# Inverse square roots of the norms: from VectorE's Newton chain to one GpSimd power instruction

## The chip, the core and the metric

The kernel runs on one core of a Trainium2 chip. The metric is the device time of one execution in microseconds (us). The core has TensorE (matrix products into PSUM), VectorE and ScalarE (which read PSUM and SBUF), GpSimd (SBUF only) and SyncE, which here only issues DMAs. The engines run side by side, each takes its own instructions in order, and they wait for each other on semaphores.

## What is computed

The input is 8 sequences of 512 tokens of 128 numbers. The model adds four residual parts: a full attention, a "local" stack, a second full attention and a gated mix. The change lies in the local stack, six layers of this (16 heads of 64, windows of 32 tokens):

```python
qkv = shift_tokens(x) @ Wqkv
q = q / max(norm(q), 1e-12) * q_scale          # per token and head
k = k / max(norm(k), 1e-12) * k_scale
q = rotate(q) * scale ; k = rotate(k) / scale  # rotary tables
attn = softmax(mask(8.0 * q @ k_window_and_previous.T))
x = (attn @ v) @ Wo + x
xn = (x - mean) / sqrt(var + 1e-5) * g + b     # of shift_tokens(x)
x = a * gelu(gate) @ W2 + b2 + x               # a, gate = split(xn @ W1 + b1)
```

Every token and head needs 1/norm(q) and 1/norm(k), and every token 1/sqrt(var + 1e-5). All of them are computed as inverse square roots of sums of squares.

## The kernel before

`local_stack` keeps the activations of all 8 sequences in SBUF and goes through 6 layers; for each layer it runs a loop over the 8 batches. One pass of that loop is called a body here, 48 of them in all, and each runs four chunks c = 0 to 3 of four heads each. The order of the work of each engine is written out by hand inside `body`, one for each engine. A chunk is a software pipeline: while the q and k of chunk c are made, the norms, broadcast and scores belong to chunk c-1, the softmax to c-2 and the value products to c-3, across the border of bodies too. The output product, the layernorm and the feed-forward part of the batch before (`prev`) go into chunks 2 and 3.

The steps of one chunk, with their lines and their engines:

- TensorE makes q (L1021) into the PSUM tile R[0], then k (L1034) into R[1], the sums of squares for each head (L1047, tiny products with `block4`) into R[3], v (L1062) into R[2], the scores (mask L1070, products L1074) into R[3], the transposes that broadcast the inverse norms (L1085, in chunk 3 also L1091) into R[0], in chunk 2 most of the output product (L1011), and the value products (L1112) into R[1]. In chunk 3 the feed-forward products (L1125, L1131) follow. `claim` makes it wait until the last reader of a tile has let go of it.
- ScalarE squares q and k (L821, L823), copies v (L829), spreads the inverse norms `rn` to `rnx` (L834), takes the exponential (L842) and copies the attention output (L849).
- VectorE rotates q (L890, `rotate(0)`), takes the norms out of PSUM (L926, in chunk 3 also L929), transposes the probabilities (L903), runs `rsqrt` (L87 to L96) on `norm`, rotates k (L890, `rotate(1)`), takes row maxima (L941), subtracts them (L943), scales the rotated q and k by the broadcast inverse norms (L954 twice, to `qn` and `kn`), and sums and inverts the softmax rows (L959, L961). `rsqrt` is a magic-number start with three Newton steps: 11 instructions that each wait for the one before. Both norms' instructions have a wait of VectorE for itself behind them, after which `norm_read` is raised.
- GpSimd forms the rotated halves from `t` into `u` (L792, L793) for q and for k, adds the squares (L794, L795), and multiplies the probabilities by the inverse sums (L801). `rotate` waits in `halves_of_pool` for `ra_ready` before it writes `t` again.
- SyncE issues eight DMAs that lay the transposed probabilities into a banded tile (L764 to L768, `pbd`) and eight for kn (L775, `kbd`).

VectorE lets TensorE have a PSUM tile again by a drain with a semaphore behind the last read (r0_dve and r1_dve in `rotate`, r3_dve behind L943, r0_dve_b behind L954; the drain at L956 is that one).

Of the kernel before, what the change touches and what calls it, by code (L numbers as in the profile page):

```python
# [11 lines left out]
ALU = mybir.AluOpType  # L12
# [3 lines left out]
D = 128  # L16
NB = 8
T = 512
NT = T // 128
LN_EPS = 1e-5  # L20
# [16 lines left out]
CH = H // NC  # L37
# [611 lines left out]
def local_stack(nc, C, xs, A):  # L649
# [8 lines left out]
    with ExitStack() as ctx:  # L658
        def sb(n, shape, dt=F32):
# [21 lines left out]
        ntmp = sb("ntmp", [D, NT * 2 * CH + NT])  # L681
        rn = sb("rn", [D, NT * 2 * CH + NT])
        NSS = NT * 2 * CH
# [17 lines left out]
                 "r2_act r0_dve r1_dve r3_dve rq_ready ra_ready sq_sum ss_ready norm_read rn_ready rnx_ready b_ready r0_dve_b "  # L701
# [81 lines left out]
        @block.gpsimd  # L783
        def _(pool):
            def body(par, l, start, b, prev):
                seen = Tally()
                for c in range(NC):
                    buf = c % 2
                    if b is not None:
                        for a in range(2):  # L790
                            pool.wait_ge(S["rq_ready"], seen.next(S["rq_ready"]))
                            nc.gpsimd.tensor_tensor(u[buf][:, 2 * a, :], t[:, 0, :], t[:, 3, :], ALU.subtract)  # L792
                            nc.gpsimd.tensor_tensor(u[buf][:, 2 * a + 1, :], t[:, 2, :], t[:, 1, :], ALU.add).then_inc(S["ra_ready"], 1)  # L793
                        nc.gpsimd.tensor_tensor(sqs[0][:], sq[0][:, 0, :], sq[0][:, 1, :], ALU.add)  # L794
                        nc.gpsimd.tensor_tensor(sqs[1][:], sq[1][:, 0, :], sq[1][:, 1, :], ALU.add).then_inc(S["sq_sum"], 1)  # L795
                        pool.drain().then_inc(S["sq_free"], 1)
                    if c == NC - 1:
                        seen.settle(pool)
                    if live(c, 2, b, prev):
                        pool.wait_ge(S["rec_ready"], seen.next(S["rec_ready"]))  # L800
                        nc.gpsimd.tensor_tensor(p[:], p[:], srec[:].unsqueeze(2).to_broadcast([D, NT * CH, 2 * WIN]),  # L801
                                                ALU.mult).then_inc(S["pn_ready"], 1)
                seen.settle(pool)

            layers(pool, body)
# [55 lines left out]
        def _(v):  # L861
# [11 lines left out]
            def body(par, l, start, b, prev):  # L873
# [12 lines left out]
                def rotate(a):  # L886
# [9 lines left out]
                    v.drain().then_inc(S["r0_dve"] if a == 0 else S["r1_dve"], 1)  # L896
# [9 lines left out]
                for c in range(NC):  # L906
# [15 lines left out]
                    if has_ss or has_var:  # L922
                        v.wait_ge(S["ss_ready"], seen.next(S["ss_ready"]))
                        lo, hi = (0 if has_ss else NSS), (NSS + NT if has_var else NSS)
                        if has_ss:
                            nc.vector.tensor_scalar(norm[:, 0:NSS], R[3][:, 0, 0:NSS], 1e-24, None, ALU.max).then_inc(S["step"], 1)  # L926
                            v.wait_ge(S["step"], seen.next(S["step"]))
                        if has_var:
                            nc.vector.tensor_scalar(norm[:, NSS:], R[3][:, 1, 0:NT], LN_EPS, None, ALU.add).then_inc(S["step"], 1)  # L929
                            v.wait_ge(S["step"], seen.next(S["step"]))  # L930
                        v.sem_inc(S["norm_read"], 1)
                    transpose_p(c)
                    if has_ss or has_var:
                        rsqrt(nc, v, seen, S["step"], norm[:, lo:hi], ntmp[:, lo:hi], rn[:, lo:hi]).then_inc(S["rn_ready"], 1)
# [3 lines left out]
                    if live(c, 2, b, prev):  # L938
# [6 lines left out]
                        v.drain().then_inc(S["r3_dve"], 1)  # L945
# [4 lines left out]
                    if has_ss:  # L950
# [5 lines left out]
                        v.drain().then_inc(S["r0_dve_b"], 1)  # L956
# [454 lines left out]
```

## Time and profile before

| | |
|---|---|
| median of 3 runs | 5786.65 us (5783.74 to 5801.6) |
| profiled execution, whole | 5801.78 us |
| its span, first to last instruction | 5800.0 us |
| TensorE busy (matmul) | 4979.5 us (86%) |
| TensorE weight loads | 2765.5 us (48%) |
| VectorE busy | 4089.1 us (71%) |
| ScalarE busy | 2198.8 us (38%) |
| GpSimd busy | 2000.6 us (34%) |
| mean granted TensorE clock | 0.929 |

The profiled execution has 1.8 us around its span. It took 15 us more than the median of the runs.

Three kinds of views are used below. The table of stretches has, for each stretch (start:end in us from the span's start), its length, the busy time of each engine with the number of instructions in it (in the order PE, PEld, DVE, ACT, POOL), the granted TensorE clock, the DMA engines' busy share and GB/s. PE is TensorE, PEld its weight loads, DVE VectorE, ACT ScalarE, POOL GpSimd. The timeline gives start, duration, engine, line, operation, output and inputs, count, and in brackets the idle time of the engine before it and what released it. The groups of instructions give the count, the busy time, the mean duration in ns, the idle time before and what ended it. The page's chain that ended last reaches only into the last few us of the program and says nothing about the local stack.

### The profile page before, as it was taken

To read this page: it belongs to the slowest core of one execution; us is meant where nothing else is said; L and a number is where in the kernel's file an instruction comes from. 1 tells how busy PE (TensorE), PEld (TensorE's weight loads), DVE (VectorE), ACT (ScalarE), POOL (GpSimd) and SP (SyncE) were. 2 spreads that over 40 slices of the span, in tenths; PEclk is the share of its full clock that TensorE was granted. 3 is DMA by queue.
4 is the path that set the end of the run, shared out by engine and by line. 5 is a ranking of instruction groups with operands and counts; after the bars stand their busy time and mean duration, and the time that the engine had idled before them with its cause. 6 is when DMAs were issued, how large, how long until landed. Compare 5 with 4: busy or idle time off the path is not lost. (4 is left out here: it accounts for less than half of the span.)

```text
span 5800.0 us, 90682 instructions
## 1 busy us (share of the span) xinstructions
PE 4979.5 (86%) x33904; PEld 2765.5 (48%) x34096; DVE 4089.1 (71%) x5868; ACT 2198.8 (38%) x2794; POOL 2000.6 (34%) x1547
## 2 busy tenths in 40 slices
PE   5999688898998999998898998998898998478886
PEld 2222255555555555555555555555555554222223
DVE  4677377777777777777777777777777776366652
ACT  0666333333333333333333333333333332035564
POOL 1111144444444444444444444444444442111110
PEclk6999799999999999999999999999999999579997
DMA  2222111112211122111222112112121111122210
GB/s 58 49 47 44 55 46 48 46 46 61 55 46 49 48 58 58 45 47 47 63 49 49 46 48 69 45 48 50 43 58 48 45 49 47 43 45 45 43 26 16
DMA packets 181029, 279.66 MB, mean 48 GB/s; under 512 B 58032, under 2 KB 79792, under 8 KB 174896
## 3 DMA queue, kind: packets, MB, share of 16 engines
q1 hardware_dynamic: 180880, 277.66, 19.5%
q8 instruction: 94, 1.54, 0.1%
q14 instruction: 55, 0.45, 0.0%
HBM read 61.70 MB, written 17.56 MB: 14 GB/s over the span
## 5 line engine op out<-in xcount | busy, mean ns | idle before, releaser
L792 POOL TENSOR_TENSOR l_u<-l_t 128x512 f32<-128x512 f32 x384 | 486.9, 1268 | 2110.3 <-DVE l_t L890 2110.3
L890 DVE SCALAR_TENSOR_TENSOR l_t<-l_r,l_qkvec,l_tab 128x1024 f32<-128x1024 f32 x768 | 949.3, 1278 | 294.5 <-ACT l_sq L821 291.3
L470 DVE TENSOR_REDUCE a_nmax<-a_pair 128x2 f32<-128x1024 f32 x512 | 612.4, 1221 | 374.5 <-PE a_pair L550 372.5
L1074 PE MATMUL l_r<-l_kbd,l_qn 128*32 128x256 f32 x12288 | 774.5, 390 | 44.5 <-DMA l_kbd<-l_kn 11.3
L388 ACT ACTIVATE a_pt<-a_st 128x512 f32<-128x512 f32 x1024 | 579.8, 597 | 335.4 <-PE a_st L534 325.3
L1021 PE MATMUL l_r<-xs,l_wqkv 128*128 (+1 forms) x768 | 431.9, 690 | 222.4 <-DVEq L956 189.0
L1074 PEld LDWEIGHTS l_r<-l_kbd,l_qn 128*32 128x32 f32 x12288 | 422.9, 111 | 302.2 <-issue 152.8
L1112 PE MATMUL l_r<-l_pbd,l_va 128*64 128x160 f32 (+1 forms) x6144 | 443.4, 297 | 127.7 <-DMA l_pbd<-l_pt 127.7
L534 PE MATMUL a_st<-a_qs,a_ks 75*128 75x512 bf16 x1024 | 391.7, 398 | 146.0 <-ACT a_pt L388 75.5
L801 POOL TENSOR_TENSOR l_p<-l_p,l_srec 128x1024 f32<-128x1024 f32 x192 | 365.3, 1903 | 415.6 <-DVE l_srec L961 284.7
L1112 PEld LDWEIGHTS l_r<-l_pbd,l_va 128*64 128x64 f32 x6144 | 400.2, 138 | 193.1 <-DVEq L896 108.3
L793 POOL TENSOR_TENSOR l_u<-l_t 128x512 f32<-128x512 f32 x384 | 489.2, 1274 | 0.0
L842 ACT ACTIVATE l_p<-l_p 128x1024 f32<-128x1024 f32 x192 | 203.1, 1058 | 721.5 <-DVE l_p L943 721.5
L1062 PE MATMUL l_r<-l_wqkv,l_xc 128*128 128x256 f32 x1536 | 424.7, 425 | 0.0
L1047 PEld LDWEIGHTS l_r<-l_block,l_sqs 128*128 128x128 f32 x3072 | 372.8, 192 | 97.7 <-issue 94.9
L550 PE MATMUL a_pair<-a_ks,a_qs 72*128 72x512 bf16 x1024 | 341.3, 419 | 83.0 <-DMA a_qs<-a_scr 59.7
L829 ACT ACTIVATE l_va<-l_r 128x1024 f32<-128x1024 f32 x192 | 196.7, 1024 | 546.0 <-PE l_r L1062 546.0
L821 ACT ACTIVATE l_sq<-l_r 128x1024 f32<-128x1024 f32 x192 | 196.6, 1024 | 538.3 <-PE l_r L1021 529.9
L1034 PE MATMUL l_r<-xs,l_wqkv 128*128 (+1 forms) x768 | 396.7, 642 | 3.0 <-DVEq L896 2.7
L534 PEld LDWEIGHTS a_st<-a_qs,a_ks 75*128 75x128 bf16 x1024 | 95.5, 97 | 561.1 <-ACT a_pt L388 429.0
L1047 PE MATMUL l_r<-l_block,l_sqs 128*128 128x4 f32 x3072 | 354.1, 247 | 1.4 <-POOL l_sqs L795 1.3
L834 ACT ACTIVATE l_rnx<-l_rn 128x1024 f32<-128x1024 f32 x192 | 203.3, 1059 | 380.5 <-DVE l_rn L96 380.5
(183 smaller groups left out, 7475.3 us busy)
## 6 DMA issues: line engine op xcount, KB each, us to landing
l_kbd<-l_kn SPq DMA_DIRECT2D x1536, 64.0 KB, 2.0
l_pbd<-l_pt SPq DMA_DIRECT2D x1344, 64.0 KB, 2.0
a_ks<-a_scr SPq DMA_DIRECT2D x96, 192.0 KB
a_qs<-a_scr SPq DMA_DIRECT2D x288, 64.0 KB
a_scr<-a_parts SPq DMA_DIRECT2D x48, 256.0 KB, 2.5
l_wqkv<-in_wqkv SPq DMA_DIRECT2D x6, 1536.0 KB, 6.9
l_pbd<-l_pt SPq DMA_DIRECT2D x192, 48.0 KB, 1.9
l_wo<-in_wo SPq DMA_DIRECT2D x6, 512.0 KB, 3.7
```

The costliest lines, as they stand in the source:

```text
L388: nc.scalar.activation(pt[n % 2][:, r, :], st[r % 2][:], ACT.Exp, scale=SC).then_inc(exp_done, 1)
L470: nc.vector.tensor_reduce(out=nmax[:, n, 2 * i:2 * i + 2], in_=pair[i][:], op=ALU.max, axis=AX.X, negate=True).then_inc(pair_dve[i], 1)
L534: nc.tensor.matmul(st[r % 2][:], ks[1 - par][0:ROWS, h, 128 * kt:128 * kt + 128], qs[1 - par][0:ROWS, h, :], start=True, stop=True).then_i ...
L792: nc.gpsimd.tensor_tensor(u[buf][:, 2 * a, :], t[:, 0, :], t[:, 3, :], ALU.subtract)
L793: nc.gpsimd.tensor_tensor(u[buf][:, 2 * a + 1, :], t[:, 2, :], t[:, 1, :], ALU.add).then_inc(S["ra_ready"], 1)
L890: last = nc.vector.scalar_tensor_tensor(out=t[:, 2 * half:2 * half + 2, :], in0=R[a][:, half, :].unsqueeze(1).to_broadcast([D, 2, T]), sca ...
L1021: last = nc.tensor.matmul(R[0][:, half, :], wqkv[par][:, o:o + D], xs[:, b, 0:T], start=True, stop=True)
L1034: last = nc.tensor.matmul(R[1][:, half, :], wqkv[par][:, o:o + D], xs[:, b, 0:T], start=True, stop=True)
L1047: last = nc.tensor.matmul(R[3][:, 0, o:o + CH], sqs[a][:, 128 * k:128 * k + 128], block4[:], start=True, stop=True)
L1062: last = nc.tensor.matmul(R[2][:, k // 2, 256 * (k % 2):256 * (k % 2) + 256], xc[:, 128 * k:128 * k + 128], wqkv[par][:, o:o + CH * DH], s ...
L1074: last = nc.tensor.matmul(R[3][q:q + 32, bank, 256 * (w // 4):256 * (w // 4) + 256], qn[:, half, WIN * W:WIN * W + WIN], kbd[half][:, :, W ...
L1112: last = nc.tensor.matmul(R[1][q:q + 64, bank, 128 * g:128 * g + WIN * span], va[cc][:, g, DH * h:DH * h + DH], pbd[c % 2][:, 0:span, o:o ...
```

## The change

A GpSimd instruction, `tensor_tensor` with ALU.pow, raises `norm` to -0.5, element by element, straight into `rn` (128x32, in chunk 3 128x36, in the tail 128x4). Its second operand is a tile of -0.5, filled once by a memset. It stands between GpSimd's halves of q and of k and waits for the new semaphore `norm_ready`, which VectorE raises with the last norm instruction. The 11 VectorE instructions of `rsqrt`, their waits and the tile `ntmp` are gone from the local stack (the layernorm passes outside keep theirs), and so are the two waits of VectorE for its own norm instructions; `norm_read` is raised by an engine no-op. The four drains of a chunk are replaced by engine no-ops that raise the same semaphores.

```diff
--- before.py
+++ after.py
@@ -678,8 +678,8 @@
         qn, kn = sb("qn", [D, 2, T]), sb("kn", [D, 2, T])
         kbd = [sb(f"kbd{i}", [D, CH, KC]) for i in range(2)]
         norm = sb("norm", [D, NT * 2 * CH + NT])
-        ntmp = sb("ntmp", [D, NT * 2 * CH + NT])
         rn = sb("rn", [D, NT * 2 * CH + NT])
+        minus_half = sb("minus_half", [D, NT * 2 * CH + NT])
         NSS = NT * 2 * CH
         rnx = sb("rnx", [D, NSS, HALF])
         p = sb("p", [D, NT * CH, 2 * WIN])
@@ -698,7 +698,7 @@
         R = [ctx.enter_context(nc.psum_tensor(f"l_r{i}", [D, 2, T], F32)) for i in range(4)]
 
         names = ("late_pe late_act late_dve late_free wqkv_free qkvec_free consts_pe consts_dve xc_ready q_dve q_act k_dve k_act v_act sq_free "
-                 "r2_act r0_dve r1_dve r3_dve rq_ready ra_ready sq_sum ss_ready norm_read rn_ready rnx_ready b_ready r0_dve_b "
+                 "r2_act r0_dve r1_dve r3_dve rq_ready ra_ready sq_sum ss_ready norm_read norm_ready rn_ready rnx_ready b_ready r0_dve_b "
                  "qn_ready kn_ready kbd_full s_ready t_ready p_ready rec_ready pn_ready pt_ready pt_free pbd_free "
                  "va_ready pv_ready ot_ready wo_ready x_ready mean_ready centred fsq_ready bc_ready xng_ready "
                  "xnf_ready g_ready a_ready gelu_ready h_ready f_ready ffn_done step pstep init mask_full").split()
@@ -782,12 +782,26 @@
 
         @block.gpsimd
         def _(pool):
+            nc.gpsimd.memset(minus_half[:], -0.5).then_inc(S["pstep"], 1)
+            pool.wait_ge(S["pstep"], 1)
+
             def body(par, l, start, b, prev):
                 seen = Tally()
+
+                def inverse_roots(has_ss, has_var):
+                    lo, hi = (0 if has_ss else NSS), (NSS + NT if has_var else NSS)
+                    pool.wait_ge(S["norm_ready"], seen.next(S["norm_ready"]))
+                    nc.gpsimd.tensor_tensor(rn[:, lo:hi], norm[:, lo:hi], minus_half[:, lo:hi], ALU.pow).then_inc(S["rn_ready"], 1)
+
                 for c in range(NC):
                     buf = c % 2
+                    has_ss, has_var = live(c, 1, b, prev), c == 3 and prev is not None
+                    if b is None and (has_ss or has_var):
+                        inverse_roots(has_ss, has_var)
                     if b is not None:
                         for a in range(2):
+                            if a == 1 and (has_ss or has_var):
+                                inverse_roots(has_ss, has_var)
                             pool.wait_ge(S["rq_ready"], seen.next(S["rq_ready"]))
                             nc.gpsimd.tensor_tensor(u[buf][:, 2 * a, :], t[:, 0, :], t[:, 3, :], ALU.subtract)
                             nc.gpsimd.tensor_tensor(u[buf][:, 2 * a + 1, :], t[:, 2, :], t[:, 1, :], ALU.add).then_inc(S["ra_ready"], 1)
@@ -893,7 +907,7 @@
                                                               in1=tab[:, 2 * a:2 * a + 2, :], op0=ALU.mult, op1=ALU.mult)
                     last.then_inc(S["rq_ready"], 1)
                     unread["ra"] = 1
-                    v.drain().then_inc(S["r0_dve"] if a == 0 else S["r1_dve"], 1)
+                    nc.vector.engine_nop().then_inc(S["r0_dve"] if a == 0 else S["r1_dve"], 1)
 
                 def transpose_p(c):
 
@@ -921,17 +935,13 @@
                     has_ss, has_var = live(c, 1, b, prev), c == 3 and prev is not None
                     if has_ss or has_var:
                         v.wait_ge(S["ss_ready"], seen.next(S["ss_ready"]))
-                        lo, hi = (0 if has_ss else NSS), (NSS + NT if has_var else NSS)
                         if has_ss:
-                            nc.vector.tensor_scalar(norm[:, 0:NSS], R[3][:, 0, 0:NSS], 1e-24, None, ALU.max).then_inc(S["step"], 1)
-                            v.wait_ge(S["step"], seen.next(S["step"]))
+                            last = nc.vector.tensor_scalar(norm[:, 0:NSS], R[3][:, 0, 0:NSS], 1e-24, None, ALU.max)
                         if has_var:
-                            nc.vector.tensor_scalar(norm[:, NSS:], R[3][:, 1, 0:NT], LN_EPS, None, ALU.add).then_inc(S["step"], 1)
-                            v.wait_ge(S["step"], seen.next(S["step"]))
-                        v.sem_inc(S["norm_read"], 1)
+                            last = nc.vector.tensor_scalar(norm[:, NSS:], R[3][:, 1, 0:NT], LN_EPS, None, ALU.add)
+                        last.then_inc(S["norm_ready"], 1)
+                        nc.vector.engine_nop().then_inc(S["norm_read"], 1)
                     transpose_p(c)
-                    if has_ss or has_var:
-                        rsqrt(nc, v, seen, S["step"], norm[:, lo:hi], ntmp[:, lo:hi], rn[:, lo:hi]).then_inc(S["rn_ready"], 1)
                     if b is not None:
                         v.wait_ge(S["k_dve"], seen.next(S["k_dve"]))
                         rotate(1)
@@ -942,7 +952,7 @@
                         v.wait_ge(S["step"], seen.next(S["step"]))
                         nc.vector.tensor_tensor(p[:], sc, smax[:].unsqueeze(2).to_broadcast([D, NT * CH, 2 * WIN]),
                                                 ALU.subtract).then_inc(S["t_ready"], 1)
-                        v.drain().then_inc(S["r3_dve"], 1)
+                        nc.vector.engine_nop().then_inc(S["r3_dve"], 1)
                     if has_var:
                         v.wait_ge(S["bc_ready"], seen.next(S["bc_ready"]))
                         nc.vector.scalar_tensor_tensor(out=xng[:], in0=xcn[:], scalar=vec[:, 4:5], in1=R[2][:, 0, :],
@@ -953,7 +963,7 @@
                         for a, (dst, ready) in enumerate(((qn, "qn_ready"), (kn, "kn_ready"))):
                             nc.vector.tensor_tensor(dst[:], u[par1][:, 2 * a:2 * a + 2, :],
                                                     R[0][:, a, :].unsqueeze(1).to_broadcast([D, 2, T]), ALU.mult).then_inc(S[ready], 1)
-                        v.drain().then_inc(S["r0_dve_b"], 1)
+                        nc.vector.engine_nop().then_inc(S["r0_dve_b"], 1)
                     if live(c, 2, b, prev):
                         v.wait_ge(S["p_ready"], seen.next(S["p_ready"]))
                         nc.vector.tensor_reduce(out=ssum[:], in_=p[:], op=ALU.add, axis=AX.X).then_inc(S["step"], 1)
```

## Rows read from the trace of the kernel before

**Rows 1.** The page, first section: busy time and share of the span.

```profile
PE 4979.5 (86%) x33904; PEld 2765.5 (48%) x34096; DVE 4089.1 (71%) x5868; ACT 2198.8 (38%) x2794; POOL 2000.6 (34%) x1547
```

**Rows 2.** Table of stretches, the whole local stack.

```profile
695.50:4937.00 4241.50, 3804.60 (x28590) 2363.32 (x28782) 3227.13 (x4902) 1480.96 (x1530) 1798.93 (x1344) 0.96 0.20 50
```

**Rows 3.** Table of stretches, chunks 0 to 3 of one body.

```profile
4619.56:4637.61 18.05, 14.68 (x138) 9.93 (x137) 15.33 (x23) 7.38 (x7) 7.47 (x6) 1.00 0.11 28
4637.61:4655.77 18.16, 14.79 (x137) 10.04 (x139) 15.31 (x23) 6.10 (x6) 9.38 (x7) 1.00 0.23 57
4655.77:4675.80 20.03, 19.80 (x150) 12.19 (x151) 16.79 (x25) 5.18 (x5) 9.62 (x8) 1.00 0.23 56
4675.80:4705.31 29.51, 28.51 (x175) 16.74 (x175) 20.17 (x31) 12.22 (x14) 11.03 (x8) 0.94 0.20 50
```

**Rows 4.** Timeline of TensorE in chunk 1 of that body.

```profile
4637.61 1.98 PE L1021 MATMUL l_r<-xs,l_wqkv 128*128 x4 [2.02 <-DVEq L956]
...
4647.20 1.97 PE L1074 MATMUL l_r<-l_kbd,l_qn 128*32 128x256 f32 x32
4649.25 1.09 PE L1085 MATMUL l_r<-ident,l_rnx 128*128 128x128 f32 x8
4651.44 2.29 PE L1112 MATMUL l_r<-l_pbd,l_va 128*64 128x160 f32 x32 [1.10 <-DMA l_pbd<-l_pt]
4655.77 1.99 PE L1021 MATMUL l_r<-xs,l_wqkv 128*128 x4 [2.04 <-DVEq L956]
```

**Rows 5.** Timeline of VectorE in the same chunk.

```profile
4643.37 0.19 DVE L926 TENSOR_SCALAR l_norm<-l_r 128x32 f32<-128x32 f32 x1
...
4644.95 0.91 DVE L87 TENSOR_SCALAR l_ntmp<-l_norm 128x32 int32<-128x32 int32 x1
...
4647.91 0.19 DVE L96 SCALAR_TENSOR_TENSOR l_rn<-l_ntmp,l_rn 128x32 f32<-128x32 f32 x1
4648.02 2.47 DVE L890 SCALAR_TENSOR_TENSOR l_t<-l_r,l_qkvec,l_tab 128x1024 f32<-128x1024 f32 x2
4650.63 1.23 DVE L941 TENSOR_REDUCE l_smax<-l_r 128x16 f32<-128x1024 f32 x1
...
4653.32 1.22 DVE L954 TENSOR_TENSOR l_qn<-l_u,l_r 128x1024 f32<-128x1024 f32 x1 [0.21 <-POOL l_u L793]
4654.46 1.21 DVE L954 TENSOR_TENSOR l_kn<-l_u,l_r 128x1024 f32<-128x1024 f32 x1
```

**Rows 6.** One line's instructions: min/median/max ns, the chain's first.

```profile
L87 DVE TENSOR_SCALAR l_ntmp<-l_norm x193: 139/901/923, 717.4 to 4933.4; 128x32 int32<-128x32 int32 x145, 128x36 int32<-128x36 int32 x47, 128x4 int32<-128x4 int32 x1
```

**Rows 7.** Timeline of GpSimd, chunk 1: the second half of q and k.

```profile
4644.54 1.28 POOL L793 TENSOR_TENSOR l_u<-l_t 128x512 f32<-128x512 f32 x1
...
4651.79 1.28 POOL L793 TENSOR_TENSOR l_u<-l_t 128x512 f32<-128x512 f32 x1
```

**Rows 8.** Timeline of SyncE's queue, start of chunk 1: kn's DMAs.

```profile
4637.54 4.94 SPq L775 DMA_DIRECT2D l_kbd<-l_kn  x8
```

**Rows 9.** Timelines of GpSimd, TensorE and VectorE in chunk 3.

```profile
4686.89 1.27 POOL L793 TENSOR_TENSOR l_u<-l_t 128x512 f32<-128x512 f32 x1
...
4690.86 1.97 PE L1074 MATMUL l_r<-l_kbd,l_qn 128*32 128x256 f32 x32
...
4693.01 1.23 DVE L941 TENSOR_REDUCE l_smax<-l_r 128x16 f32<-128x1024 f32 x1
```

**Rows 10.** Table of stretches, chunks 1 and 2 of another body.

```profile
2541.04:2560.72 19.68, 16.42 (x138) 10.64 (x139) 15.32 (x23) 6.10 (x6) 9.37 (x7) 0.91 0.21 53
2560.72:2582.29 21.57, 21.42 (x149) 12.77 (x151) 16.12 (x25) 5.19 (x5) 10.47 (x8) 0.92 0.23 57
```

**Rows 11.** Groups of GpSimd's instructions: a two-input one and the shortest.

```profile
L801 POOL TENSOR_TENSOR l_p<-l_p,l_srec 128x1024 f32<-128x1024 f32 x192 | 365.3, 1903 | 415.6 <-DVE l_srec L961 284.7 <-POOLq L63 130.9
...
L1403 POOL MEMSET const-float32-0.0<- 128x1 f32 x1 | 0.1, 104 | 0.3 <-issue 0.3
```

**Rows 12.** Timeline of ScalarE in chunk 1: the copy of rn.

```profile
4648.14 1.06 ACT L834 ACTIVATE l_rnx<-l_rn 128x1024 f32<-128x1024 f32 x1 [2.25 <-DVE l_rn L96]
```

## The prediction

> **What bounds the kernel now.** I read the page first: TensorE is busy 86% of the span, VectorE 71%, GpSimd 34% [rows 1]. An average over stages says little here, so the second view is the table of stretches. The local stack, the only code that the change touches, is 4241.5 us of the 5800.0 [rows 2]. Inside it one batch of one layer (a "body") has four chunks of heads. The third view cuts one body at the starts of its q products (L1021): chunks of 18.05, 18.16, 20.03 and 29.51 us, 85.75 us together [rows 3]. TensorE is busy nearly all of chunks 2 and 3 (19.80 of 20.03, 28.51 of 29.51), but only 14.7 to 14.8 us of chunks 0 and 1. So chunks 0 and 1 end by something else. The reader is to see which.
>
> The fourth view is the timeline of chunk 1, engine by engine. TensorE starts q at 4637.61, ends the scores (L1074) at 4647.20 + 1.97 = 4649.17, transposes the broadcast norms (L1085) from 4649.25, waits 1.10 us for a DMA before the value products (L1112), ends those at 4651.44 + 2.29 = 4653.73, and waits 2.04 us for VectorE's drain at L956 [rows 4]. VectorE meanwhile works without a pause: norms (L926), the transpose, the Newton chain from 4644.95 to 4647.91 + 0.19 = 4648.10, the k rotation (L890), row maxima (L941), and qn and kn (L954), the last of which ends at 4654.46 + 1.21 = 4655.67 [rows 5]. The next q starts 0.10 us behind that. The loop of chunks 0 and 1 is therefore kn, q, ScalarE's square, VectorE's whole list, kn. The scores had been ready at 4649.17, but row maxima start at 4650.63: VectorE is 1.46 us late there, behind the 3.15 us of the Newton chain.
>
> **The Newton chain, removed.** It has 11 instructions and takes 4648.10 - 4644.95 = 3.15 us of VectorE per chunk, in 192 chunks [rows 5, 6]. Its first instruction takes 0.91 us here, with a minimum of 0.14 in the group; it ends at 4645.86, just behind GpSimd's L793 (4644.54 + 1.28 = 4645.82) [rows 5 to 7]. So 0.7 us of the chain are a wait for GpSimd inside an instruction. The Trainium skill (SBUF — State Buffer on-chip working memory, SBUF: two separate sides) calls the port pair of VectorE and GpSimd "an exclusive lock, not a bandwidth split" for VectorE operations in a two-port mode; by that rule, the trace agrees. The new power instruction would not be held by it either, since VectorE's neighbours (L890, L941) read PSUM or one SBUF input.
>
> The saving does not come whole. Three things become next late.
> First, the k rotation waits for GpSimd's halves of the q rotation (ra_ready), done at 4645.82. Now the chain covers that wait. It would start at 4645.87 instead of 4648.02 and end near 4648.35.
> Second, row maxima wait for the scores: 4649.17 and some 0.05 for the signal, 4649.22. The 0.9 us between are idle time. That is 1.41 us earlier than 4650.63.
> Third, from row maxima to the end of kn VectorE needs 4655.67 - 4650.63 = 5.04 us, of which 0.21 is a wait for GpSimd's L793 [rows 5]. That wait goes, as the two k halves are done by 4648.40 + 2 x 1.28 = 4651.0 [rows 7], before qn at 4651.7. So kn ends at 4649.22 + 4.83 = 4654.05, 1.62 us earlier.
> The value products have their DMA at about the old time, since the transpose that feeds it comes ahead of the chain. They end at 4653.7 or, if the transpose moves up by the wait that goes in front of it, near 4653.5, and the q product at 4654.15 still waits 0.6 us. The DMAs of kn (eight issues, 4.94 us, [rows 8]) start with kn's end and are followed by scores 7.4 us behind q, the same distance as before, so they move along and cost nothing; with a cover of some half a microsecond if they land 2 us behind the last issue.
> Chunk 0 has the same list in the same order: also 1.6 us. Chunk 2 is TensorE's from end to end: only the 0.06 us in which the L1085 transposes wait for ScalarE's copy of rn. In chunk 3 the scores end at 4690.86 + 1.97 = 4692.83 and row maxima start at 4693.01 [rows 9]: 0.13 us. Sum: 1.61 + 1.62 + 0.06 + 0.13 = 3.42 us a body.
>
> **The clock.** TensorE's granted clock is at the lower of its two levels (1.2 GHz against 2.4) for part of some chunks: the body of [rows 10] has chunks of 19.68 and 21.57 us at 0.91 and 0.92 where [rows 3] has 18.16 and 20.03 at 1.00. In both the engine stood 2.0 us before q. Over the whole stack the clock is 0.96 [rows 2]: 8% of 4241.5 us, 339 us, at the lower level. Chunk 3 alone explains 0.06 x 2 x 29.51 x 48 = 170 us [rows 3], whose cause (norm matmuls of 1 and 4 columns) stays. The other 169 us are those of chunks 1 and 2 and cost half of themselves, 85 us, or 1.7 us a body. I take all of this as won, because the wait of 2.04 us falls to 0.6 and the one of 1.10 to 0.9. This is a judgement; its ends are 0 and 1.7.
>
> **The power instruction, added.** One GpSimd operation on 128x32 (128x36 in chunk 3) between the q halves and the k halves, free to start when L793 ends (norms are ready 2 us before). No row shows a power. Below: GpSimd's shortest operation, 0.10 us [rows 11], plus 36 elements at the 2.5 ns of L793: 0.2 us. Above: if it cost as the Newton chain would on GpSimd, 11 passes of 0.73 us (0.64 fixed, from the 1.27 us for 512 elements [rows 7] against 1.90 for 1024 in L801 [rows 11], and 0.09), 8 us. I take 1.0 us, ten passes inside one instruction, nearer to the low end since one instruction is issued once. What it may cost without harm, from L793's end at 4645.82: ScalarE's copy needs 0.05 + 1.06 [rows 12] before the transposes at 4649.20, so 2.2 us (2.2 in chunks 0 to 2; in chunk 3, L793 ends at 4686.89 + 1.27 = 4688.16 [rows 9], 3.5 us). In chunks 0 and 1 late transposes are covered a while by the DMA wait, and the k halves by the wait for scores: 3.3 us. In chunk 2 every microsecond over 2.2 moves TensorE.
>
> **The no-ops.** Four drains a chunk become engine no-ops. A drain shows as the 0.14 us between the k rotation's second half (4648.02 + 2.47 = 4650.49) and L941 at 4650.63, where kn, with no drain in front, starts 0.08 before qn ends [rows 5]. Two of them are on the loop of chunks 0 and 1 (before qn, behind kn). Between +0.1 and -0.1 us each, 2 x 2 x 47.5 x 0.1 = 19 us either way; I take 0, as it is not known when the no-op signals. The one memset more is nothing.
>
> **The sum.** 3.42 + 1.7 = 5.1 us a body, 47.5 bodies (the first and the last are partial): 242 us. The profiled execution took 5801.8 us (1.8 around its span of 5800.0), 15 above the median of the runs; most of what differs can be clock, which the change takes away, so I keep the result: 5801.8 - 242 = 5560 us.
>
> **Rivals.**
> *The power is slow.* With a price P from L793's end, a body loses (P - 3.3) twice, (P - 2.2) and (P - 3.5); against 3.36, the 3.42 less what chunk 2 gave (no clock is won when TensorE waits for the norms) it decides at P = 3.9 us, 110 ns an element. At P = 5: 1.7 x 2 + 2.8 + 1.5 - 3.35 = 4.4 us a body, 209 us, 6010 us, slower; at the bound of 8 about 6580. For it: a power is a logarithm, a product and an exponential in software; against it: 36 elements only. The Trainium skill (GPSIMD Engine Reference, Instruction dispatch) puts a first call of freshly loaded code at about 6 us; paid once, the sum would be 5566; paid in each chunk, it is this rival at P = 7. No run here shows it.
> *The power is middling*, 2.2 to 3.9 us: 5640 to 5800, with P = 3 at 5801.8 - 47.5 x (3.42 - 0.8) = 5677, without the clock's part.
> *The clock stays.* 3.42 x 47.5 = 162 us: 5640.
> *Nothing moves.* Some wait that the chain covered now (a release by no-op that comes late, the landing of kn's DMAs) stands where VectorE's list stood: 5785.
>
> **Chances.** Forecast 0.52; clock stays 0.13; middling power 0.10; slow power 0.20; nothing moves 0.05. The forecast's own range is 5520 (no-ops gain, the median's 15 us hold) to 5600. The range to hold 8 in 10 goes to the middling power's end, 5800. A difference of 0.3% (17 us) is what measurement can tell. Faster: 0.52 + 0.13 + 0.09 = 0.74; same 0.06; slower 0.20.
>
> **What would show it.** In the profile after: VectorE some 192 x 2.8 = 540 us less busy (the chain's 3.15 less its short gaps); row maxima idle before them with TensorE's L1074 as releaser, some 0.9 us in chunks 0 and 1; L1021's wait on VectorE's queue near 0.6 us; chunks of 16.4, 16.5, 20.0, 29.4 us at clock 1.00, 1.00, 1.00, 0.94. Wrong if the power lasts over 2.2 us (then L1085 waits for ScalarE's L834, and that for GpSimd), if chunk 1 or 2 still shows clocks near 0.91, or if L1021 waits as long as before.

## The result, and the profile after

The changed kernel takes 6178.6 us (median of 4 runs, 6156.6 to 6191.6) against 5785.2 us beside it: 1.067 times the time of the kernel before, 95% interval 1.063 to 1.071. The forecast was 5560 us. The rival "the power is slow" is what came.

The page of the profile after, its busy line and its three heaviest rows on GpSimd and TensorE (the columns are those of [rows 1] and [rows 11]):

```profile
PE 5038.7 (82%) x33904; PEld 2871.0 (47%) x34096; DVE 3548.2 (58%) x3745; ACT 2196.4 (36%) x2794; POOL 3063.9 (50%) x1741
...
L794 POOL TENSOR_TENSOR l_rn<-l_norm,l_minus_half 128x32 f32<-128x32 f32 (+1 forms) x193 | 1078.0, 5586 | 28.4 <-POOLq L63 21.2
...
L1095 PE MATMUL l_r<-ident,l_rnx 128*128 128x128 f32 x1536 | 266.7, 330 | 660.5 <-ACT l_rnx L848 660.5
...
L848 ACT ACTIVATE l_rnx<-l_rn 128x1024 f32<-128x1024 f32 x192 | 202.7, 1056 | 1079.7 <-POOL l_rn L794 1079.7
```

VectorE is 540.9 us less busy (4089.1 in [rows 1]), as it should be. GpSimd is 1063 us more busy, and the 193 power instructions, 5.6 us each on the mean, are all of that. Read the two right-hand columns from the bottom up: ScalarE's copy to rnx waited 1080 us for the power, and TensorE's L1095 transposes waited 660 us for the copy. (In the changed kernel L807 is the old L793, L848 the old L834, L904 the rotation L890, L951 and L953 are L941 and L943, L964 is L954, and L1031, L1084, L1095 and L1122 are TensorE's L1021, L1074, L1085 and L1112.)

The same chain in chunk 1 of one body. Timelines of GpSimd, ScalarE, TensorE and VectorE, cut to it:

```profile
3561.57 1.28 POOL L807 TENSOR_TENSOR l_u<-l_t 128x512 f32<-128x512 f32 x1
3562.81 5.44 POOL L794 TENSOR_TENSOR l_rn<-l_norm,l_minus_half 128x32 f32<-128x32 f32 x1
...
3568.28 1.05 ACT L848 ACTIVATE l_rnx<-l_rn 128x1024 f32<-128x1024 f32 x1 [5.36 <-POOL l_rn L794]
...
3564.23 1.97 PE L1084 MATMUL l_r<-l_kbd,l_qn 128*32 128x256 f32 x32
3569.39 1.09 PE L1095 MATMUL l_r<-ident,l_rnx 128*128 128x128 f32 x8 [3.19 <-ACT l_rnx L848]
3570.41 3.96 PE L1122 MATMUL l_r<-l_pbd,l_va 128*64 128x160 f32 x32
...
3566.28 1.23 DVE L951 TENSOR_REDUCE l_smax<-l_r 128x16 f32<-128x1024 f32 x1 [0.85 <-PE l_r L1084]
...
3570.82 1.22 DVE L964 TENSOR_TENSOR l_qn<-l_u,l_r 128x1024 f32<-128x1024 f32 x1 [2.05 <-POOL l_u L807]
3571.95 1.21 DVE L964 TENSOR_TENSOR l_kn<-l_u,l_r 128x1024 f32<-128x1024 f32 x1
```

The line of L951 answers to L941 in [rows 5]: row maxima now wait 0.85 us for the scores, as forecast. The path is L807, power, L848, L1095, L1122, q. L1122 takes 3.96 us here where [rows 4] has 2.29, because TensorE's clock is at its lower level. At 2.29 us it would have ended at 3572.70, and kn, whose k halves on GpSimd stand behind the power, would have been last, at 3573.16. So in this chunk the power holds up two ways to the next q that end within half a microsecond of each other, and the clock decides that it is TensorE's. The stretches of that body, chunks 0 to 3 (columns as in [rows 3]):

```profile
3535.15:3554.65 19.50, 16.17 (x139) 11.17 (x138) 13.42 (x13) 6.47 (x6) 12.82 (x7) 0.91 0.11 26
3554.65:3574.31 19.66, 16.32 (x140) 11.40 (x139) 12.68 (x13) 6.10 (x6) 14.73 (x8) 0.91 0.21 53
3574.31:3597.44 23.13, 19.80 (x152) 12.17 (x151) 12.68 (x13) 6.10 (x6) 16.64 (x9) 1.00 0.25 61
3597.44:3631.04 33.60, 29.12 (x176) 17.65 (x176) 17.28 (x20) 12.22 (x14) 15.44 (x8) 0.90 0.14 35
```

Against [rows 3] each chunk is longer, by 1.45, 1.50, 3.10 and 4.09 us. The body of [rows 3] is one at the full clock in chunks 1 and 2. Over the 47 whole bodies of each trace (start of the first q to start of the next body's) the means are 87.17 us before and 95.30 after: 8.13 x 48 = 390 us, which is about the loss of 393.

The wait alone does not say which clock follows. L1095 waits 3.18, 3.19 and 3.19 us in chunks 0, 1 and 2; chunks 0 and 1 are at 0.91, chunk 2 is at 1.00, and so they are on the mean of all bodies. One thing that differs in chunk 2 is that most of the output product, 5.3 us of it, stands between L1095 and L1122.

### The profile page after: what moved, and what is told of

The parts are those of the page before. It is cut to its first block and busy times, and to the rows that moved or that the text cites. A ratio compares the mean times of both kernels' runs of the same rounds, so it can differ in the third digit from the quotient of the medians.

```text
span 6154.8 us, 88804 instructions
## 1 busy us (share of the span) xinstructions
PE 5038.7 (82%) x33904; PEld 2871.0 (47%) x34096; DVE 3548.2 (58%) x3745; ACT 2196.4 (36%) x2794; POOL 3063.9 (50%) x1741
## 5 line engine op out<-in xcount | busy, mean ns | idle before, releaser
L904 DVE SCALAR_TENSOR_TENSOR l_t<-l_r,l_qkvec,l_tab 128x1024 f32<-128x1024 f32 x768 | 950.5, 1279 | 604.9 <-ACT l_sq L835 336.0
L794 POOL TENSOR_TENSOR l_rn<-l_norm,l_minus_half 128x32 f32<-128x32 f32 (+1 forms) x193 | 1078.0, 5586 | 28.4 <-POOLq L63 21.2
L1095 PE MATMUL l_r<-ident,l_rnx 128*128 128x128 f32 x1536 | 266.7, 330 | 660.5 <-ACT l_rnx L848 660.5
L1084 PE MATMUL l_r<-l_kbd,l_qn 128*32 128x256 f32 x12288 | 759.5, 385 | 37.1 <-DMA l_kbd<-l_kn 8.4
L1122 PE MATMUL l_r<-l_pbd,l_va 128*64 128x160 f32 (+1 forms) x6144 | 610.9, 370 | 3.2 <-DMA l_pbd<-l_pt 3.2
L848 ACT ACTIVATE l_rnx<-l_rn 128x1024 f32<-128x1024 f32 x192 | 202.7, 1056 | 1079.7 <-POOL l_rn L794 1079.7
L1122 PEld LDWEIGHTS l_r<-l_pbd,l_va 128*64 128x64 f32 x6144 | 532.4, 180 | 110.7 <-issue 79.8
L1095 PEld LDWEIGHTS l_r<-ident,l_rnx 128*128 128x128 f32 x1536 | 208.5, 167 | 752.8 <-ACT l_rnx L848 752.8
L1084 PEld LDWEIGHTS l_r<-l_kbd,l_qn 128*32 128x32 f32 x12288 | 418.6, 109 | 280.5 <-issue 127.1
L807 POOL TENSOR_TENSOR l_u<-l_t 128x512 f32<-128x512 f32 x384 | 490.2, 1277 | 0.0
L863 ACT ACTIVATE l_ot<-l_r 128x1024 f32<-128x1024 f32 x192 | 196.4, 1023 | 787.0 <-PE l_r L1122 787.0
L1031 PE MATMUL l_r<-xs,l_wqkv 128*128 (+1 forms) x768 | 384.7, 623 | 39.0 <-DVEq L883 25.5
L964 DVE TENSOR_TENSOR l_qn<-l_u,l_r 128x1024 f32<-128x1024 f32 x192 | 234.2, 1220 | 314.3 <-POOL l_u L807 195.1
L349 POOL CAST a_rparts<-a_rows 8x512 bf16<-8x512 f32 x32 | 19.3, 603 | 788.3 <-ACT a_rows L398 788.3
L1072 PE MATMUL l_r<-l_wqkv,l_xc 128*128 128x256 f32 x1536 | 380.8, 391 | 0.0
```

Of the source, the lines that this page charges most:

```text
L794: nc.gpsimd.tensor_tensor(rn[:, lo:hi], norm[:, lo:hi], minus_half[:, lo:hi], ALU.pow).then_inc(S["rn_ready"], 1)
L904: last = nc.vector.scalar_tensor_tensor(out=t[:, 2 * half:2 * half + 2, :], in0=R[a][:, half, :].unsqueeze(1).to_broadcast([D, 2, T]), sca ...
L1031: last = nc.tensor.matmul(R[0][:, half, :], wqkv[par][:, o:o + D], xs[:, b, 0:T], start=True, stop=True)
L1072: last = nc.tensor.matmul(R[2][:, k // 2, 256 * (k % 2):256 * (k % 2) + 256], xc[:, 128 * k:128 * k + 128], wqkv[par][:, o:o + CH * DH], s ...
L1084: last = nc.tensor.matmul(R[3][q:q + 32, bank, 256 * (w // 4):256 * (w // 4) + 256], qn[:, half, WIN * W:WIN * W + WIN], kbd[half][:, :, W ...
L1095: last = nc.tensor.transpose(R[0][:, a, 128 * k:128 * k + 128], rnx[:, o:o + CH, :].rearrange("p h i -> p (h i)"), C["ident"][:])
```

## The experiments

Each was timed beside the kernel before. Ratios are to that kernel.

### One part of the change at a time

The no-ops alone, in the kernel before:

```diff
-  v.drain().then_inc(S["r0_dve"] if a == 0 else S["r1_dve"], 1)
+  nc.vector.engine_nop().then_inc(S["r0_dve"] if a == 0 else S["r1_dve"], 1)
-  v.drain().then_inc(S["r3_dve"], 1)
+  nc.vector.engine_nop().then_inc(S["r3_dve"], 1)
-  v.drain().then_inc(S["r0_dve_b"], 1)
+  nc.vector.engine_nop().then_inc(S["r0_dve_b"], 1)
```

> The kernel before with only the four drains of a chunk made engine no-ops; the Newton chain stays on VectorE. Theory A (all of the loss is the length of the power instruction, 5.4 us for 32 columns and 6.1 for 36 in the profile after): no loss here. In the profile after, the norms start 0.08 us before the q rotation ends, where a drain had put 0.13 us between them; but in this kernel the chain's first instruction waits for GpSimd's second half and qn waits for it again, so little of that reaches the end: 5765 to 5790 us, against 5785 before. Theory B (the hand-over by no-ops is dear, because a release comes late): TensorE's wait for q grows from 2.0 us, and the kernel takes 5800 us or more.

Measured: 5721.8 us, 0.986 (0.983 to 0.989). Both theories miss, B in its direction and A in its size. The no-ops bring 71 us, and nothing in the prediction held that much. It is taken up below.

The change without its no-ops: drains in place of all five of them. (The kernel before had four; the fifth, at `norm_read`, replaces the wait that stood there.)

```diff
-  nc.vector.engine_nop().then_inc(S["norm_read"], 1)
+  v.drain().then_inc(S["norm_read"], 1)
...
```

> The changed kernel with drains again in place of its no-ops; only the power instruction is left of the change. Theory A: 6165 to 6200 us, as the changed kernel (6178), since chunks are bound by the path power, ScalarE's copy, L1095 transposes, value products, q, on which no drain lies except the one behind the q rotation (0.2 us a chunk at most, 40 us in all if every bit counted). Theory B: at least 50 us faster than the changed kernel.

Measured: 6170.6 us, 1.065 (1.061 to 1.069). Theory A. The no-ops have no part in the loss. What is left is the power instruction and the handing of the roots to GpSimd, and the next run parts these two.

### The forecast without the power's price

A product of two constant tiles stands in the power's place. It leaves out the inverse roots and keeps every wait and release.

```diff
-  nc.gpsimd.tensor_tensor(rn[:, lo:hi], norm[:, lo:hi], minus_half[:, lo:hi], ALU.pow).then_inc(S["rn_ready"], 1)
+  nc.gpsimd.tensor_tensor(rn[:, lo:hi], minus_half[:, lo:hi], minus_half[:, lo:hi], ALU.mult).then_inc(S["rn_ready"], 1)
```

> The changed kernel with a product of two constant tiles in place of the power, at the same place, of the same size, with the same waits and releases: the inverse roots are left out and rn is 0.25 everywhere. It measures the forecast without the power's price. Theory A: my sum holds, 5560 us (5520 to 5600), row maxima wait some 0.9 us for the scores, q waits some 0.6 us for VectorE, and chunks 1 and 2 are at the full clock. Theory C (the hand-over of the roots to another engine costs the gain whatever the instruction lasts: GpSimd's queue, ra_ready ahead of the k rotation): 5700 us or more. Theory D (the clock is not won): 5640 us.

Measured: 5540.2 us, 0.957 (0.953 to 0.960). Theory A; C and D fall. The product lasts 0.24 us. The changed kernel differs from this one in that instruction alone and takes 638 us more, so the whole loss, and the gain that did not come, are the power's length and what TensorE's clock made of it. The stretches of one body:

```profile
2399.43:2415.80 16.37, 14.77 (x140) 9.94 (x138) 12.53 (x13) 7.29 (x7) 7.67 (x7) 1.00 0.13 31
2415.80:2432.27 16.47, 14.87 (x139) 10.04 (x139) 12.35 (x13) 6.20 (x7) 9.58 (x8) 1.00 0.25 63
2432.27:2452.15 19.88, 19.88 (x151) 12.18 (x151) 13.65 (x14) 5.40 (x6) 11.47 (x9) 1.00 0.27 65
2452.15:2481.56 29.41, 28.64 (x176) 16.91 (x175) 17.29 (x20) 12.22 (x14) 9.56 (x8) 0.94 0.18 44
```

The prediction had 16.4, 16.5, 20.0 and 29.4 at clocks 1.00, 1.00, 1.00 and 0.94. And the waits of chunk 1, on the timelines of VectorE and TensorE:

```profile
2424.10 2.47 DVE L904 SCALAR_TENSOR_TENSOR l_t<-l_r,l_qkvec,l_tab 128x1024 f32<-128x1024 f32 x2 [1.41 <-POOL l_u L807]
2427.43 1.22 DVE L951 TENSOR_REDUCE l_smax<-l_r 128x16 f32<-128x1024 f32 x1 [0.86 <-PE l_r L1084]
...
2429.13 2.29 PE L1122 MATMUL l_r<-l_pbd,l_va 128*64 128x160 f32 x32 [0.76 <-DMA l_pbd<-l_pt]
2432.27 1.13 PE L1031 MATMUL l_r<-xs,l_wqkv 128*128 x2 [0.85 <-DVEq L966]
```

The three things that the prediction called next late stand there: the k rotation behind GpSimd's q halves, row maxima behind the scores, and a shorter wait of q for VectorE. Of the 3.15 us of the chain, 1.4 became the first wait and 0.86 the second.

### How long the power may last

The power on the first 8, 16 or 24 columns and the product on the rest. The other inverse roots are left out.

```diff
-  nc.gpsimd.tensor_tensor(rn[:, lo:hi], norm[:, lo:hi], minus_half[:, lo:hi], ALU.pow).then_inc(S["rn_ready"], 1)
+  mid = lo + min(8, hi - lo)
+  if mid < hi:
+      nc.gpsimd.tensor_tensor(rn[:, mid:hi], minus_half[:, mid:hi], minus_half[:, mid:hi], ALU.mult)
+  nc.gpsimd.tensor_tensor(rn[:, lo:mid], norm[:, lo:mid], minus_half[:, lo:mid], ALU.pow).then_inc(S["rn_ready"], 1)
```

> The changed kernel with the power on the first 8 columns only and the product of constants on the rest, so most inverse roots are left out. From the durations of the changed kernel (1.0 us for 4 columns, 5.4 for 32, 6.1 for 36: 0.3 us and 0.16 to 0.17 a column) the power lasts 1.6 us and the pair 1.85, under the 2.2 us that my sum said are free. Theory A (thresholds as in the sum): the time of the cheap kernel, 5540 us, within 15. Theory E (no cover: each microsecond of GpSimd in a chunk counts from the first one): 1.6 us x 192 = 300 us more, 5840.

> As before with 16 columns: the pair lasts about 3.1 us, over the 2.2 of chunk 2 and under the 3.3 and 3.5 of the others. Theory A: chunk 2 alone grows, by 0.9 us, 43 us in all: 5570 to 5600. Theory E: 5540 + 2.9 x 192 = 6100.

> As before with 24 columns: the pair lasts about 4.3 us. Theory A: chunks 0 and 1 grow by 1.0 each, chunk 2 by 2.1, chunk 3 by 0.8, 4.9 us a body, 235 us: 5775, and up to 80 more if TensorE's clock falls behind the longer waits, so 5775 to 5860: about where the kernel before stands. Theory E: 6300.

The power's instructions in these runs (minimum, median and maximum ns), for 8, 16 and 24 columns:

```profile
L797 POOL TENSOR_TENSOR l_rn<-l_norm,l_minus_half x193: 1007/1647/1668, 711.6 to 4685.4; 128x8 f32<-128x8 f32 x192, 128x4 f32<-128x4 f32 x1
```

```profile
L797 POOL TENSOR_TENSOR l_rn<-l_norm,l_minus_half x193: 1008/2912/2931, 724.4 to 4692.8; 128x16 f32<-128x16 f32 x192, 128x4 f32<-128x4 f32 x1
```

```profile
L797 POOL TENSOR_TENSOR l_rn<-l_norm,l_minus_half x193: 1006/4175/4193, 716.7 to 4999.2; 128x24 f32<-128x24 f32 x192, 128x4 f32<-128x4 f32 x1
```

| columns by power | power, us | us from L807's end, about | chunks 0, 1, 2, 3 of one body, us | median, us | ratio |
|---|---|---|---|---|---|
| 0 | none | 0.24 | 16.37, 16.47, 19.88, 29.41 | 5540.2 | 0.957 |
| 8 | 1.65 | 1.9 | 16.37, 16.47, 19.88, 29.38 (medians) | 5550.5 | 0.959 |
| 16 | 2.91 | 3.1 | 16.37, 16.47, 20.78, 28.26 | 5542.8 | 0.958 |
| 24 | 4.18 | 4.4 | 18.44, 17.50, 22.03, 31.13 | 5847.7 | 1.010 |
| all (the change) | 5.44, in chunk 3 6.1 | 5.4 | 19.50, 19.66, 23.13, 33.60 | 6178.6 | 1.067 |

Theory A, and theory E falls: with 8 columns no chunk is longer, so the first 1.9 us cost nothing. The thresholds of chunks 0 to 2 are where the sum had them. At 3.1 us chunk 2 alone grows, by 0.90 us. At 4.4 us chunk 1 grows by 1.03 (4.4 - 3.3 = 1.1) and chunk 2 by 2.15 (4.4 - 2.2 = 2.2). Break-even lies between 3.1 and 4.4 us, where the rival had put 3.9.

Three entries show the clock instead. With 16 columns chunk 3 is 1.15 us shorter than with none, so the whole was some 30 us under what I expected:

```profile
2473.01:2501.27 28.26, 26.82 (x175) 15.69 (x175) 17.28 (x20) 12.23 (x14) 12.41 (x9) 1.00 0.18 43
```

Its clock is 1.00 where 0.94 stood in each body shown before. The prediction had said that the cause of chunk 3's low clock, the norm products of 1 and 4 columns, stays. They are in this chunk too, as long as before (1.84 us for the 16 of 4 columns and 1.03 for the 8 of one), and the clock did not fall: they alone are not the cause. With 24 columns chunk 0 is 2.07 us longer where 1.1 are due, at a clock of 0.91, and chunk 3 is 1.72 longer where 0.9 are due, at 0.95. In that run L1098, the transposes, wait 2.08 us in chunk 0 as in chunk 1, and chunk 1 is at 1.00. Again equal waits, and different clocks behind them.

### Another home for the roots

```diff
+  act.wait_ge(S["norm_ready"], seen.next(S["norm_ready"]))        # ahead of the copy of v
+  nc.scalar.activation(lnorm[:, lo:hi], norm[:, lo:hi], ACT.Ln).then_inc(S["rn_ready"], 1)
...
-  nc.scalar.activation(rnx[:], rn[:, 0:NSS].unsqueeze(2).to_broadcast([D, NSS, HALF]), ACT.Copy)
+  nc.scalar.activation(rnx[:], lnorm[:, 0:NSS].unsqueeze(2).to_broadcast([D, NSS, HALF]), ACT.Exp, scale=-0.5)
```

> The changed kernel with the inverse roots on ScalarE: logarithm of the 32 or 36 norms ahead of the copy of v, and the copy to rnx replaced by the exponential of -0.5 times the logarithm; no power on GpSimd. It adds two table loads of 1.28 us a chunk on ScalarE, which waited 2.5 us before the copy of v and 2.3 us behind it. Theory A (the roots only have to be there when the scores end): rnx is ready 1 us before the scores end, so the time is that of the kernel with the cheap instruction within 20 us, near 5560 us. If ScalarE's loads fall on the path (rnx later than the scores), TensorE's L1095 waits for it in chunks 2 and 3 and the time is 5600 to 5700 us.

Measured: 5543.7 us, 0.957 (0.954 to 0.961), with all of the computation in it. It beats both kernels and equals the cheap instruction within 4 us. ScalarE and TensorE in chunk 1:

```profile
2428.05 1.28 ACT L832 ACT_TABLE_LOAD   x1
2429.34 0.23 ACT L832 ACTIVATE l_lnorm<-l_norm 128x32 f32<-128x32 f32 x1
2430.52 1.02 ACT L835 ACTIVATE l_va<-l_r 128x1024 f32<-128x1024 f32 x1 [0.95 <-PE l_r L1065]
2431.64 1.28 ACT L842 ACT_TABLE_LOAD   x1
2432.93 1.06 ACT L842 ACTIVATE l_rnx<-l_lnorm 128x1024 f32<-128x1024 f32 x1
...
2432.85 1.97 PE L1077 MATMUL l_r<-l_kbd,l_qn 128*32 128x256 f32 x32
2434.75 1.09 PE L1088 MATMUL l_r<-ident,l_rnx 128*128 128x128 f32 x8
```

ScalarE spends 2.8 us more a chunk than for the copy alone, two table loads among it, and in chunk 1 all of it lies in gaps; the chunk lengths of this kernel (16.37, 16.47, 19.88 and 29.41 us in the median) are those with the cheap instruction. rnx is ready at 2433.99, 0.8 us before the scores end at 2434.82. The Trainium skill (ScalarE: Activation LUTs, Table sets: the hidden batching unit) says that logarithm and exponential share one set; in this build each got its own load. The same page of the Trainium skill (What ACT_TABLE_LOAD costs) has about 1283 ns for a load, which the trace agrees with, and about 2.66 us with a drain for every switch of sets, which it does not: the logarithm starts 1.32 us behind the end of the squares before the load (2428.02 to 2429.34).

### What the no-ops are worth

Drains in place of all five no-ops in the kernel with the cheap instruction (inverse roots left out):

```diff
-  nc.vector.engine_nop().then_inc(S["r3_dve"], 1)
+  v.drain().then_inc(S["r3_dve"], 1)
...
```

> The kernel with the cheap instruction, inverse roots left out, and drains again in place of the no-ops. The kernel before with no-ops alone was 71 us faster. If the no-ops are worth as much here (theory F), 5600 to 5620. If they are worth only what they take from the path (theory A: in chunks 0 and 1 one drain, of 0.14 to 0.2 us, ahead of qn), 5550 to 5565, and the rest of the 71 us was TensorE's clock, which here is already at the full level in chunks 1 and 2.

Measured: 5573.0 us, 0.963 (0.960 to 0.967). Theory F falls. By the medians they are worth 33 us here, somewhat over theory A's 10 to 25. The runs of either kernel spread over 33 to 39 us, so the chunk lengths are the firmer ground. The two gaps on the path, ahead of qn and behind kn, read on VectorE's timeline of chunk 1, first with drains:

```profile
2449.01 1.22 DVE L953 TENSOR_TENSOR l_p<-l_r,l_smax 128x1024 f32<-128x1024 f32 x1
2450.43 1.22 DVE L964 TENSOR_TENSOR l_qn<-l_u,l_r 128x1024 f32<-128x1024 f32 x1 [0.21 <-issue]
```

and with no-ops:

```profile
2428.69 1.22 DVE L953 TENSOR_TENSOR l_p<-l_r,l_smax 128x1024 f32<-128x1024 f32 x1
2429.84 1.22 DVE L964 TENSOR_TENSOR l_qn<-l_u,l_r 128x1024 f32<-128x1024 f32 x1
```

qn starts 0.20 us behind the end of L953 with a drain between and 0.07 before it with a no-op: 0.27 us a chunk. Behind kn it is little: the next q starts 0.10 us after its end with a drain and 0.08 with a no-op. Chunks 0 and 1 are 0.31 longer with drains (16.68 and 16.78), 2 x 0.31 x 48 = 30 us, which is about the 33.

In the kernel with the Newton chain the no-ops brought 71 us. One of them alone:

```diff
-  v.drain().then_inc(S["r3_dve"], 1)
+  nc.vector.engine_nop().then_inc(S["r3_dve"], 1)
```

> The kernel before with one of its four drains a chunk made a no-op, the one between the subtraction of the maxima (L943) and qn (L954). In the kernel before qn starts 0.20 us behind L943 and 0.25 us behind GpSimd's second half, so the drain and not GpSimd is what it waited for. Theory F1 (this drain alone is on the loop of chunks 0 and 1): both get 0.17 us shorter as with all four no-ops, 16 us in all from the path, and whatever the clock gives on top as in that run: 5720 to 5775. Theory F2 (the gain of the four no-ops came from the others): 5785 to 5795, no change.

Measured: 5725.8 us, 0.988 (0.985 to 0.990). F1: this drain is as good as all of the effect. Its direct part is 0.17 us in each of chunks 0 and 1 (medians 17.90 and 18.00, where [rows 3] has 18.05 and 18.16), 16 us. The other 50 are TensorE's clock: it cost chunks 1 and 2 of all bodies 85 us in the kernel before and 22 here (half of the time at the lower level, from the granted clock of each chunk). TensorE's q products (L1021; busy us and mean ns of one, then the idle time before them and its releasers) with all four no-ops and with this one:

```profile
L1021 PE MATMUL l_r<-xs,l_wqkv 128*128 x672 | 349.7, 645 | 168.5 <-DVEq L956 164.4 <-issue 4.1
```

```profile
L1021 PE MATMUL l_r<-xs,l_wqkv 128*128 x672 | 337.3, 625 | 155.0 <-DVEq L956 150.7 <-issue 4.2
```

In the kernel before that mean is 689 ns with a wait of 163 us. Of its 768 q products 140 last over 0.75 us (the others 0.59), against 68 and 38 here, and 16 with the cheap instruction. With four no-ops the slow products fell by half while the wait ahead of q stayed at 2.0 us in chunks 1 and 2. With the one no-op that wait fell too, to 1.85, so this run does not part the two.

Is it the drain or the body's length that the clock follows? One attempt, in the kernel before:

```diff
   v.drain().then_inc(S["r3_dve"], 1)
+  nc.vector.memset(scratch[:], 0.0)
```

> The kernel before, all its drains kept, with one idle VectorE instruction more a chunk, a memset of 128x128 on a tile that nobody reads, between L943's drain and qn. Nothing is left out. It makes the loop of chunks 0 and 1 some 0.1 to 0.2 us longer and leaves TensorE's wait for q at 2.1 to 2.2 us. Theory G (the share of bodies in which q and k run at the lower clock hangs on the body's length, to tenths of a microsecond, and not on the drains): slow q products, 140 of 768 in the kernel before and 68 with the no-ops, change by tens, and the time differs from 5785 by more, or otherwise, than the 10 to 20 us that the instruction puts on the path. Theory H (the clock was lost to the drains or to the length of the wait): about 140 slow products or a few more, and 5795 to 5810 us.

Measured: 5789.5 us, 0.999 (0.998 to 1.001), 126 slow q products. It says little: the memset took 0.17 us, but chunks 0 and 1 grew by 0.02 us each (medians 18.08 and 18.19), a fifth of what I wanted or less. So neither theory is decided. Why bodies that are 0.3 to 0.4 us shorter lose the clock half as often, or less, stays open.

## Why the prediction was wrong

**What bounds the kernel: right.** In chunks 0 and 1 it was VectorE's list and in chunks 2 and 3 TensorE. The cheap instruction showed it, chunk by chunk, within 0.15 us.

**The Newton chain, removed: right in its steps, and in size with the no-ops' help.** The sum had 3.42 us a body and a body of 82.3 us at full clock in chunks 0 to 2; the cheap kernel's is 82.13. That it comes out so well is in part luck. One reading in it was wrong: the 0.21 us in front of qn, which the view puts down to GpSimd's L793 [rows 5], were the drain's. L793 had ended at 4651.79 + 1.28 = 4653.07 [rows 7], while L943 in front of the drain ended at 4653.12. The same 0.21 us stand in the cheap kernel with drains, with nothing of GpSimd's due: there its two k halves were done about 0.8 us before L953 ended. So the chain alone gives 1.4 us in each of chunks 0 and 1 (18.06 and 18.17 us in the median before, 16.68 and 16.78 in the cheap kernel with drains) where the sum had 1.61 and 1.62. The no-ops, counted as nothing, gave 0.31 more in each and covered it.

**The clock: right in size where the sum applied it.** With the cheap instruction chunks 1 and 2 are at 1.00, slow q products fall from 140 to 16, and 5540 us is 20 under the forecast. The lower clock cost chunks 1 and 2 85 us before, as the sum had it, and 10 in the cheap kernel. The reason given, that the wait for q falls from 2.0 to 0.6 us, is not shown. It fell to 0.85, but with four no-ops in the kernel before the wait stayed at 2.0 and half of the slow products went as well. The cause named for the low clock of chunk 3, the norm products, does not hold alone: with 16 columns by power they are all there, and chunk 3 is at 1.00. What the prediction did not count is that a slow power loses the clock again, in chunks 0, 1 and 3.

**The power instruction, added: wrong, and this is the step that failed.** Its price was taken as 1.0 us between bounds of 0.2 and 8. It is 5.44 us for 32 columns and 6.14 for 36: 0.158 us a column (5.44 - 1.65 over 24 columns) and 0.4 us besides. I took ten passes at the 2.5 ns of an addition. In that measure a column costs 63. How the instruction computes a power no run shows, so the argument of a logarithm, a product and an exponential stays untested. The bounds held the truth, and no row stood near it on either side. Yet 0.52 + 0.13 of the chances went to a price under 2.2 us. With bounds 40 times apart, a decision point of 3.9 us inside them and no row between, the chances should have lain nearer to even, and the range should have reached the rival.

**The rival's own price: right in shape, too low in size.** "The power is slow" by its formula gives at 5.44 and 6.14 us 2 x 2.14 + 3.24 + 2.64 = 10.2 us a body over the cheap one, and as a whole about 6125 us where 6179 came. Measured are 3.13, 3.19, 3.25 and 4.19, together 13.8 in the bodies shown. Chunk 2, at the full clock, is exact. The 3.6 us left over are TensorE's clock in the other three. In chunk 1, with L1122 at 2.29 us, the next q would have started 0.1 us behind kn, at 3573.26, a chunk of 18.61 us: 2.14 over the cheap one, as the formula has it. In chunk 0 L1095 takes 1.59 for 1.09 and L1122 3.41 for 2.29; in chunk 3, after a wait of 4.3 us, 1.97 and 3.29. The rival counted no clock as won, but also none as lost.

**The no-ops: mis-sized.** Taken as 0 within 19 us. They are worth 33 us with the chain gone and 71 with it. The gap of 0.20 us before qn could be read in [rows 5], had it not been put down to GpSimd, and 0.27 us come back there, since without the drain the next instruction starts before the last one ends. In the changed kernel they do little (6178.6 against 6170.6 us without them): there both ways to the next q go through the power, and VectorE waits 2.05 us ahead of qn.

The first use of the power cost nothing extra: it starts at 704.51, as L807 ends, lasts 5.46 us, and the next instruction starts before it ends. So the 6 us for a first call of freshly loaded code, which the prediction cited from the Trainium skill (GPSIMD Engine Reference, Instruction dispatch), were not seen here.

## What to carry to other kernels

An operation that no row of the trace shows is priced by one run of it alone before it is put into a chain; between bounds 40 times apart the middle is no estimate. Work out first how long the new instruction may last for free and where it turns to a loss: here 2.2 and 3.3 us, which held, and 3.9, which lies between the 3.1 and 4.4 us that were run. One look at these beside bounds of 0.2 and 8 us would have been a reason to try ScalarE's gaps as well, which came out 4.3% faster than before. And when a view names a releaser, look at when that one ended: one that was done earlier hides a drain or the engine's own issue.

## What the runs showed of the hardware that I had not expected

- GpSimd's power costs 0.158 us for each column of 128 elements: 1.01 us for 4 columns, 1.65 for 8, 2.91 for 16, 4.18 for 24, 5.44 for 32. A product of 32 columns at the same place takes 0.24 us.
- A VectorE drain with a semaphore, between two instructions of 1.22 us, costs 0.27 us against an engine no-op that raises the same semaphore.
- A change of 0.17 us in two chunks, with TensorE's wait in front of q at 1.85 us instead of 2.0, cut the products at the lower clock from 140 to 38 of 768 and was worth 50 us beyond its path.
- Equal waits of TensorE were followed by different clocks: 3.2 us in chunks 0, 1 and 2 of the changed kernel by 0.91, 0.91 and 1.00, and 2.08 us in chunks 0 and 1 with 24 columns by 0.91 and 1.00.
